# A graph layer and a mixture of experts on one core: one-hot windows of 7 nodes instead of 8, and the second biases as one bf16 product

## The reference

```python
def rgcn(x, basis, comp, root, bias):          # twice, with relu behind each
    W = einsum('rb,bde->rde', comp, basis)      # 8 relations from 4 bases
    h = einsum('nd,rde->nre', x, W)
    seg = dst * 8 + edge_type
    sums = segment_sum(h[src, edge_type], seg, n * 8)
    cnt = segment_sum(1, seg, n * 8)
    return (sums / maximum(cnt, 1)).reshape(n, 8, -1).sum(1) + x @ root + bias
h = relu(rgcn(relu(rgcn(layernorm(x), ...0)), ...1))
x = x + (h @ lin_w[t] + lin_b[t] for each node's type t)
xn = layernorm(layernorm(x)) * gamma + beta
logits = xn @ Wr + br                           # 8 experts, the best two
w_full = softmax over the best two, 0 elsewhere # [N, 8]
for e in range(8):
    y += (gelu(xn @ W1[e] + b1[e]) @ W2[e] + b2[e]) * w_full[:, e]
out = x + y
```

## Time and profile before

| | |
|---|---|
| median of 3 runs | 4539.33 us |
| profiled execution, its own time | 4543.36 us |
| its span, first to last instruction | 4541.6 us |
| mean granted clock of TensorE | 0.791 |
| TensorE busy | 3709.3 us, 82% |
| VectorE busy | 3406.6 us, 75% |
| GpSimd busy | 3237.3 us, 71% |
| ScalarE busy | 885.4 us, 19% |

### The profile page before, as it was taken

How to read it: one execution, slowest core, us unless ns; L and a number is a source line. 1 busy time by engine, 2 the same in 40 slices (tenths; PEclk the granted TensorE clock), 3 DMA queues, 4 the chain that set the end, 5 groups by cost and what they waited for, 6 DMA issues and landing times.

```text
span 4541.6 us, 123466 instructions
## 1 busy us (share of the span) xinstructions
PE 3709.3 (82%) x38021; PEld 3256.7 (72%) x38022; DVE 3406.6 (75%) x9952; ACT 885.4 (19%) x2488; POOL 3237.3 (71%) x3388
## 2 busy tenths in 40 slices
PE   2576676766776776766559999999999999999999
PEld 2455555555555555555449999999999999999998
DVE  6688888888888888888746766767676767767674
ACT  5000000000000000000003333333333333333333
POOL 1777777777777777777577777777777777777770
PEclk6565665665655665665659999999999999999999
DMA  7666656655556555556466665555655566555661
GB/s 230 177 190 198 178 167 170 169 167 170 168 168 169 166 170 170 166 170 170 130 172 173 174 172 169 167 169 167 170 168 170 171 171 171 167 171 167 171 171 20
DMA packets 358895, 762.08 MB, mean 168 GB/s; under 512 B 130103, under 2 KB 182108, under 8 KB 358657
## 3 DMA queue, kind: packets, MB, share of 16 engines
q0 software_dynamic: 215360, 663.86, 51.1%
q1 hardware_dynamic: 129381, 81.62, 6.9%
q10 hardware_dynamic: 14112, 16.06, 1.0%
HBM read 725.50 MB, written 35.78 MB: 168 GB/s over the span
## 4 chain that ended last, share of the span: by engine, by line
PE 59%; POOL 13%; issue 12%; DMA 10%; DVE 3%; SPq 1%; ACT 0%; POOLq 0%; DVEq 0%; ACTq 0%
PE bank L1514 16%; PE bank L1527 15%; POOL slot L614 13%; PE bank L1427 11%; DMA slot<-table,idx 7%; PE bank L1459 7%; PE bank L1423 3%; PE bank L1489 3%; PE bank L1490 2%; DMA off<-off_d 2%; DVE inv L1079 1%; PE bank L1455 1%; PE bank L1586 1%; SPq L456 0%; SPq L457 0%
## 5 line engine op out<-in xcount | busy, mean ns | idle before, releaser
L614 POOL DMA_INDIRECT slot<-table,idx x3354 | 3215.3, 959 | 1121.7 <-issue 956.0
L1427 PE MATMUL bank<-hot,slot 128*128 (+1 forms) x21168 | 1236.9, 211 | 61.2 <-DMA slot<-table,idx 54.8
L1427 PEld LDWEIGHTS bank<-hot,slot 128*128 128x128 bf16 x21168 | 993.9, 108 | 122.7 <-issue 67.2
L1423 PE MATMUL bank<-hot,ones_b 128*128 x1764 | 398.4, 226 | 651.0 <-DMA slot<-table,idx 364.5
L1423 PEld LDWEIGHTS bank<-hot,ones_b 128*128 128x128 bf16 x1764 | 181.1, 103 | 924.1 <-issue 865.0
L1514 PE MATMUL bank<-root_sb,ffn_w 128*128 128x128 f32 x6272 | 772.3, 278 | 0.0
L1527 PE MATMUL bank<-ffn_w,act 128*128 128x256 f32 x3136 | 757.9, 385 | 1.0 <-DVE root_sb L1173 0.7
L1514 PEld LDWEIGHTS bank<-root_sb,ffn_w 128*128 128x128 f32 x6272 | 740.8, 192 | 8.0
L1046 DVE SCALAR_TENSOR_TENSOR bank<-scaled,small,bank 128x128 f32<-128x128 f32 x2352 | 665.1, 352 | 20.8
L1527 PEld LDWEIGHTS bank<-ffn_w,act 128*128 128x128 f32 x3136 | 569.3, 190 | 65.4 <-issue 1.1
L1025 DVE SCALAR_TENSOR_TENSOR mixed<-scaled,comp_sb,mixed 128x256 f32<-128x256 f32 x1372 | 573.5, 481 | 10.5
(11 more groups left out here) (159 smaller groups left out, 2562.0 us busy)
## 6 DMA issues: line engine op xcount, KB each, us to landing
slot<-table,idx POOLq DMA_INDIRECT x3354, 3.1
inv<-inv_d SPq DMA_DIRECT2D x98, 256.0 KB
table<-ffn_w SPq DMA_DIRECT2D x7, 1344.0 KB, 5.9
table<-parts ACTq DMA_DIRECT2D x49, 192.0 KB
ffn_w<-in_L_ffn_W_dram SPq DMA_DIRECT2D x16, 512.0 KB, 5.9
typed_x_d<-zn ACTq DMA_DIRECT2D x49, 128.0 KB
zn<-in_x_dram SPq DMA_DIRECT2D x48, 128.0 KB
root_sb<-typed_x_d SPq DMA_DIRECT2D x48, 128.0 KB
```

The source lines that it names most:

```text
L614: gp.indirect_dma_start(out=slot[:, k, :], out_offset=None, in_=table[layer], in_offset=bass.IndirectOffsetOnAxis(ap=idx[:, h, k:k + 1], a ...
L1423: t.matmul(C[:, at], ones_b[:, :], oh, start=(k == 0), stop=(k == TILES - 1), skip_group_check=True)
L1427: last = t.matmul(S[f][:, at], slot[:, k, q * D + f * P:q * D + (f + 1) * P], oh, start=(k == 0 and q == 0), stop=(k == TILES - 1 and q == ...
```

## The change

Two edits.

1. **SPAN is 7 instead of 8.** A tile's window is 56 slots wide instead of 64 (COLS), so `hot`, the one-hot instructions and the tile matmuls have 56 columns per tile; the windows are placed anew, the last one at 512 - 56.
2. **The bias product is one bf16 matmul.** `take_weights` splits the routing weights exactly into three bf16 parts (w = w0 + w1 + w2) and writes them three times, as three stripes of 32 columns [w0 w1 w2 and 8 zeros], into `wf_parts`. A bf16 matmul with a bf16 identity turns all 96 columns at once, and ScalarE copies the 96 x 128 result as bf16 over `wfT`. `b2_parts` holds in stripe j the j-th bf16 part of `b2`, three times. One bf16 product over the 96 rows then sums the nine products of parts. `split_b2` makes `b2_parts` once, at the beginning of the first layer; SP loads `b2` nine times, into an unused piece of `scaled`.

```diff
-SPAN = 8
+SPAN = 7
@@
-        b2_sb = sb("b2_sb", [P, D], F32)
+        b2_sb = scaled[:, 1, :, :, :].rearrange("p a r n -> p (a r n)")[:, HALVES * R * P - D:]
@@
+        wf_parts = sb("wf_parts", [P, PARTS, 32], BF16)
+        wf_rest = sb("wf_rest", [P, EXPERTS], F32)
+        b2_parts = sb("b2_parts", [PARTS * 32, D], BF16)
+        ident_b = sb("ident_b", [P, P], BF16)
+        wfT_b = wfT[0:PARTS * 32, 0:P // 2].bitcast(BF16)
+        b2_mid = wfT[0:PARTS * 32, :].bitcast(BF16)
@@ SP, start
-            sp.dma_start(b2_sb[0:EXPERTS, :], b2).then_inc(weights_in, 16)
+            for j in range(PARTS):
+                for i in range(PARTS):
+                    at = j * 32 + i * EXPERTS
+                    sp.dma_start(b2_sb[at:at + EXPERTS, :], b2).then_inc(weights_in, 16)
@@ ScalarE
-                    sc.activation(wfT[0:EXPERTS, :], T2[0:EXPERTS, 256:256 + P], ACT.Copy).then_inc(wfT_done, 1)
+                    sc.activation(wfT_b, T2[0:PARTS * 32, 256:256 + P], ACT.Copy).then_inc(wfT_done, 1)
@@ VectorE
             def take_weights(p):
-                v.tensor_tensor(wfull[:, 0, :], wfull[:, 2, :], wfull[:, 1, :], ALU.add).then_inc(wf_done, 1)
+                ch.link(v.tensor_tensor(wfull[:, 0, :], wfull[:, 2, :], wfull[:, 1, :], ALU.add))
+                wide = [P, PARTS, EXPERTS]
+
+                def part(i):
+                    return wf_parts[:, :, i * EXPERTS:(i + 1) * EXPERTS]
+                ch.link(v.tensor_copy(part(0), wfull[:, 0, :].unsqueeze(1).broadcast_to(wide)))
+                ch.link(v.tensor_tensor(wf_rest[:, :], wfull[:, 0, :], wf_parts[:, 0, 0:EXPERTS], ALU.subtract))
+                ch.link(v.tensor_copy(part(1), wf_rest[:, :].unsqueeze(1).broadcast_to(wide)))
+                v.tensor_tensor(part(2), wf_rest[:, :].unsqueeze(1).broadcast_to(wide), part(1),
+                                ALU.subtract).then_inc(wf_done, 1)
@@
+            def split_b2():
+
+                rows_ = slice(0, PARTS * 32)
+                v.tensor_copy(ident_b[:, :], ident[:, :])
+                ch.link(v.tensor_copy(b2_parts[rows_, :], b2_sb[rows_, :]))
+                ch.link(v.tensor_tensor(b2_sb[rows_, :], b2_sb[rows_, :], b2_parts[rows_, :], ALU.subtract))
+                ch.link(v.tensor_copy(b2_mid, b2_sb[rows_, :]))
+                v.tensor_copy(b2_parts[32:64, :], b2_mid[32:64, :])
+                v.tensor_tensor(b2_parts[64:96, :], b2_sb[64:96, :], b2_mid[64:96, :],
+                                ALU.subtract).then_inc(b2_split, 1)
@@ first_layer()
                 one_hots(1, 0)
+                split_b2()
@@ TensorE, dense()
-                    t.transpose(T2[0:EXPERTS, 256:256 + P], wfull[:, 0, :], ident[:, :]).then_inc(wfT_ps, 1)
+                    t.matmul(T2[0:PARTS * 32, 256:256 + P], wf_parts[:, :, :].rearrange("p j c -> p (j c)"),
+                             ident_b[:, :], start=True, stop=True).then_inc(wfT_ps, 1)
@@
-                    t.matmul(T[:, 0:D], wfT[:, :], b2_sb[:, :], start=True, stop=True).then_inc(b2_ps, 1)
+                    t.matmul(T[:, 0:D], wfT_b, b2_parts[:, :], start=True, stop=True).then_inc(b2_ps, 1)
@@ weights_ready()
+                pe.wait_ge(b2_split, 1)
```

More of the change, by code:

```diff
@@ L316, in build @@
         b2_ps = sem("b2_ps")
+        b2_split = sem("b2_split")
         b2_added = sem("b2_added")
         out_done = sem("out_done")
-        N_WEIGHTS = 13
+        N_WEIGHTS = 12 + PARTS * PARTS
         matched = sem("matched")
@@ L580, in _ @@
             gp.iota(pid[:, :], [[0, 1]], base=0, channel_multiplier=1, allow_small_or_imprecise_dtypes=True)
-            for z in (linb_sb, b2_sb, tmaskT, wfT):
+            for z in (linb_sb, b2_sb, tmaskT):
                 gp.memset(z[:, :], 0.0)
+            gp.memset(wf_parts[:, :, :], 0.0)
             gp.memset(ident[:, :], 0.0).then_inc(s_const, 1)
@@ L1274, in second_layer @@
                 base = ch.base + ch.n
-                per = 5 + 4 + (R - 1)
+                per = 5 + 4 + 4 + (R - 1)
                 with dve.Fori(1, PAIRS // 2) as p2:
```

## The result

The kernel after takes 4496.56 us, the median of four runs (4494.21 to 4497.35), beside 4538.80 for the kernel before on the same chip (4537.16 to 4543.28): 42.2 us less, ratio 0.9909 [0.9896, 0.9921]. The forecast was 48 us less, 4491; the time lies in the range. An undisturbed gather (the median one of the first layer, 300 to 2200 us) takes 0.949 us in the profiles of the kernel before, e6, e7 and e8, and 0.946 or 0.947 in the ten others, whatever the kernel: over a layer that gathers bound this makes some 5 us, and no run shows why.

What follows compares the result with a forecast made beforehand. GpSimd's gathers bound the first layer, TensorE the second, with GpSimd 1.3 us per pair behind. From the profiled 4543.4: -31.6 - 18.9 - 0.6 + 0.6 + 2 = -48.5, so 4494.9; against the median 4491 us, range 4481 to 4523.

Steps and rivals of the forecast that it cites:

- Where the time comes from: Savings come in the TensorE-bound second layer, 0.6 us in its last two steps; the gather-bound first layer gives nothing.
- The tile group: Second layer, 18 bf16 matmuls: column streaming at 56 columns saves 57 ns a group, 558 groups, 31.6 us (0 to 36).
- a bf16 load keeps the array 13 ns: TensorE tile matmuls: a bf16 weight load holds the array some 13 ns, well below the 29 ns per matmul.
- The bias product: Second layer on TensorE: 0.52 us falls to 0.11, saving 0.41 in 46 pairs, 18.9 us.
- the transpose: Routing-weight transpose on TensorE, now bf16: +0.01 us, 46 times, +0.6 us (-2 to +5).
- the four new instructions: VectorE in take_weights: four more linked instructions, 0.85 us per pair (0.7 to 1.9), hidden, so costing nothing.
- the slack before the last down projection: VectorE's sixth expert sum: slack falls from 0.83 to 0.2 us, barely holding; if not, 5 to 9 us lost.
- The mixing: VectorE's last eight mixing products end 3.7 us before TensorE needs them, so added VectorE work there costs nothing.
- The pair: Second layer, TensorE's time for a pair of blocks: 44.57 us falls to 43.49.
- Gathers, 2 us for single waits: Second layer: GpSimd's gathers, 1.272 us each, end in a tie with TensorE; 2 us charged for single waits.
- Rival 2: Second layer: gathers become the bound, two casts holding GpSimd up 0.38 us per pair; 4507 us, chance 0.08.
- The start at nothing: Start: eight more b2 copies on SP (2.7 us) and split_b2 (2.9 us) hidden, costing nothing; without cover 5.6 us.

Runs made afterwards that it cites:

- e6: Kernel before with SPAN = 4 (32-column tiles), edges outside the narrower windows left out: 4506.42 us, 37.6 less than the kernel before.
- e7: Kernel after with the first layer's mixing summed in SBUF in place of PSUM: 4542.47 us, 1.6 less than the kernel before.
- e8: Kernel after with b2 loads moved behind the first two blocks' tables and both routing-weight casts done five times: 4496.52 us, 47.5 less than the kernel before.
- e1: Kernel before with SPAN = 7 alone, the bias product left in fp32: 4508.06 us, 29.8 less than the kernel before.
- e9: Kernel after, unchanged, measured again in a later comparison: 4499.45 us, 37.8 less than the kernel before.
- e10: Kernel after with b2 loads moved behind the first two blocks' tables, measured again: 4498.11 us, 39.2 less than the kernel before.
- e11: Kernel after with late b2 loads and both routing-weight casts done five times, measured again: 4490.06 us, 47.2 less than the kernel before.

## Why the prediction was right, and where its steps were off

- *Where the time comes from* held. First to last basis product of the second layer: 2134.2 us before, 2090.8 after, -43.4; the steps behind the last one 64.4 and 63.8, -0.6 as predicted. The first layer gave nothing by the change: it is 5.6 us shorter in the profile after (2143.5 and 2137.9), and 2142.9 in e6 with the narrowest tiles, so this goes with the undisturbed gather, 0.949 and 0.946 us in the two profiles. That the profiled 4496.87 lies within 2 us of the predicted 4494.9 is luck by that much; the medians, 4496.56 and 4491, tell the miss of 6.
- *The tile group* was sized right, 0.058 us against 0.057, for a reason that holds only at these widths. The estimate that a bf16 load keeps the array 13 ns leaves the floor out: at 32 columns 25 ns remain, by the load or by something else. And one group of the twelve, between the typed layers, gains nothing (0.65 us before, 0.67 after), so 11 x 0.058 x 46 = 29 us came in place of 31.6. e1 measured 29.8.
- *The bias product* is exact: 0.11 us, 0.41 saved. So are the transpose (+0.02 for +0.01), the four new instructions (0.88 for 0.85) and the slack before the last down projection, 0.2 us. The mixing ended 2.6 us before its basis product, in place of 3.7 before: covered, even with 1.7 us more.
- *The pair*: 43.56 us where 43.49 stood. The 0.07 is the twelfth group and the transpose; 46 times that is 3 us.
- *Gathers, 2 us for single waits*: 4.0 in this profile, 6.2 in e9. The mechanism was the right one (a tie, lost in the pairs with one gather more), the pace 1.275 and not 1.272. Rival 2 named the wrong instructions: the casts cost nothing, the mixing that had been there before costs 0.8 us of gathers a pair (by the fit 30 us in the 1600 from 2650 us on).
- *The start at nothing* was wrong: 2.3 us. It looked at room in the queue, not at when the store behind it lands.
- Together: 48.5 - 3 (pair) - 2 (waits beyond the 2) - 2.3 (start) = 41, beside the measured 42.2 and 37.8.

## What to carry to other kernels

When a gain brings a second engine within 1% of the first, ask what stretches that engine's instructions and when, not only how long they are on average; moving other work by a microsecond or two can then be worth more than removing some. Before narrowing a matmul further, measure the floor with a narrower one, whatever it leaves out. A queue that is idle hides the issue of a load, but not what the load does to the next store that someone waits for.

## What the runs showed of the hardware that was not expected

- A load-and-matmul pair in bf16 with 128 weight columns takes 29.2, 25.9 and 25.2 ns with 64, 56 and 32 columns (18 in a row, at a granted clock of 1.00).
- VectorE instructions with both inputs in SBUF stretch GpSimd's gathers beside them (0.950 to 0.971 us on average over a layer, e8 and e7); the same instructions with one input in PSUM don't, and are as fast.
- Useless instructions on VectorE made the kernel 8 us faster than the one without them (e10 and e11, side by side).
- The group of tile matmuls between f32 matmuls of the typed layers takes 0.67 us with 56 columns and 0.68 with 32 (2918.68 to 2919.36 in e6), elsewhere 0.46 and 0.45: there something other than width sets it, which no run looked into.
